# Three edits at the joint of two stages: where keys are finished, cached rows gathered, and last projections made

## What is computed

```python
# selective scan, from x_dbl = u @ x_proj_w.T
delta = softplus(delta_r @ dt_proj_w.T + dt_proj_b)
h_t = exp(delta_t * A) * h_{t-1} + (delta_t * u_t) * B_t     # per channel and state
y_t = sum_n(h_t * C_t) + u_t * D
x1  = x + y
# attention on x1
q, k = rope(rms(x1 @ Wq.T)), rope(rms(x1 @ Wk.T));  v = x1 @ Wv.T
k_blocks[blk, :, off, :], v_blocks[blk, :, off, :] = k, v    # new rows into the cache
o = softmax(mask(q @ k_all.T * SCALE)) @ v_all
```

## Time and profile before

| what | value |
|---|---|
| time, median of 3 runs | 1906.23 us (1903.25 to 1907.43) |
| span of the profiled execution, first to last instruction | 1905.3 us |
| PE busy | 1825.1 us, 96% |
| DVE busy | 1455.5 us, 76% |
| ACT busy | 1261.5 us, 66% |
| POOL busy | 1268.7 us, 67% |
| mean granted TensorE clock, share of full speed | 0.991 |

### The profile page before, as it was taken

One profiled execution on the slowest core, in us unless ns is written; L12 is line 12 of the kernel. 1 busy time (PEld: TensorE's weight loads), 2 busy tenths in 40 slices (PEclk: granted clock), 3 DMA queues, 4 the chain that ended last, 5 costly groups with the idle time before them and its releaser, 6 DMA issues.

```text
span 1905.3 us, 30000 instructions
## 1 busy us (share of the span) xinstructions
PE 1825.1 (96%) x9311; PEld 1271.2 (67%) x9311; DVE 1455.5 (76%) x2572; ACT 1261.5 (66%) x3942; POOL 1268.7 (67%) x1255
## 2 busy tenths in 40 slices
PE   6899999999999999988899899999999999999998
PEld 6777777777777777666355575756657575665764
DVE  8999999999999999999456675655657565565522
ACT  5888888888888888866356664655647465564621
POOL 5789999999999999988777654544545554450000
PEclk9999999999999999999899999999999999999999
DMA  5323323332333223321777434334343434431021
GB/s 207 146 113 146 146 96 124 146 135 107 124 147 146 111 112 143 133 78 67 227 205 216 115 103 126 106 106 129 99 127 105 117 113 111 124 89 60 30 69 38
DMA packets 117741, 230.67 MB, mean 121 GB/s; under 512 B 31364, under 2 KB 70292, under 8 KB 112464
## 3 DMA queue, kind: packets, MB, share of 16 engines
q1 hardware_dynamic: 84496, 163.48, 24.3%
q0 software_dynamic: 33088, 65.28, 12.7%
HBM read 212.09 MB, written 44.70 MB: 135 GB/s over the span
## 4 chain that ended last, share of the span: by engine, by line
PE 46%; ACT 3%; issue 1%; DVE 1%; DMA 1%; POOL 0%; ACTq 0%; DVEq 0%; SPq 0%; POOLq 0%
PE attn_psum L1974 12%; PE attn_psum L1990 12%; PE attn_psum L1904 5%; PE attn_psum L1891 4%; PE attn_psum L1884 4%; PE attn_psum L1931 3%; PE attn_psum L1875 2%; PE attn_psum L2008 2%; PE attn_psum L1865 1%; PE attn_psum L1916 1%; ACT xh L1615 1%; ACT th L1616 1%; ACT prob L1572 0%; DMA kv_at<-kv_scratch,new_now 0%; PE attn_psum L1954 0%
## 5 line engine op out<-in xcount | busy, mean ns | idle before, releaser
L1040 DVE TENSOR_TENSOR_SCAN hid<-scan_psum,dbu 128x1024 f32<-128x1024 f32 x256 | 581.8, 2273 | 1.4 <-ACT scan_psum L672 1.4
L1212 PE MATMUL scan_psum<-hid,ident 128*128 128x256 f32 x2048 | 520.3, 385 | 27.7 <-POOL hid L513 27.5
L1212 PEld LDWEIGHTS scan_psum<-hid,ident 128*128 128x128 f32 x2048 | 379.5, 191 | 189.4 <-issue 106.4
L1726 DVE CUSTOM_DVE_ANT_0 prob<-attn_psum,mask 128x336 f32<-128x336 f32 x256 | 119.8, 505 | 269.4 <-PE attn_psum L1884 269.4
L513 POOL TENSOR_TENSOR hid<-hid,kv_at 128x1024 f32<-128x1024 f32 x128 | 306.1, 2405 | 26.8 <-DVE hid L1040 26.4
L513 POOL TENSOR_TENSOR hid<-hid,bc 128x1024 f32<-128x1024 f32 x128 | 306.0, 2403 | 24.1 <-DVE hid L1040 23.6
L1578 ACT COPY p_t<-attn_psum 112x384 f32<-112x384 f32 x256 | 122.5, 487 | 274.8 <-PE attn_psum L1891 274.8
L1990 PE MATMUL attn_psum<-w,ffn_hid 128*128 128x512 f32 x512 | 238.5, 595 | 5.0 <-DVE y_sb L1791 5.0
L1504 POOL DMA_INDIRECT kv_at<-kv_scratch,new_now x189 | 200.9, 1063 | 60.8 <-issue 57.3
L1974 PE MATMUL attn_psum<-xs_in,w 128*128 128x256 f32 x1024 | 232.4, 381 | 7.5 <-ACT xs_in L1584 6.6
L672 ACT ACTIVATE scan_psum<-kv_at,neg_a 128x252 f32<-128x252 f32 x512 | 211.6, 466 | 10.7 <-DVE hid L1040 9.6
(11 more groups left out here) (229 smaller groups left out, 3034.4 us busy)
## 6 DMA issues: line engine op xcount, KB each, us to landing
bc<-bc_scratch SPq DMA_DIRECT2D x16, 2048.0 KB, 7.5
kv_at<-bc_scratch SPq DMA_DIRECT2D x15, 2048.0 KB, 7.4
q_scratch<-qg SPq DMA_DIRECT2D x32, 260.0 KB, 2.0
early<-q_scratch SPq DMA_DIRECT2D x32, 260.0 KB
x_pair<-in_x_pairs SPq DMA_DIRECT2D x32, 256.0 KB, 2.9
kv_scratch<-kvg SPq DMA_DIRECT2D x32, 256.0 KB, 2.1
a_scratch<-a_sb SPq DMA_DIRECT2D x32, 256.0 KB, 3.5
w_o<-x_scratch SPq DMA_DIRECT2D x32, 256.0 KB, 3.4
```

Of the source, the lines that this page charges most:

```text
L1040: nc.vector.tensor_tensor_scan(hid[:, k % RING, :, :].rearrange("p n t -> p (n t)"), decay[k % 2], dbu[:, k % RING, :, :].rearrange("p n t ...
L1212: mm = nc.tensor.matmul(yc, ident[:], hid[:, k % RING, i, :], start=False, stop=(k % 4 == 3 and i == 3))
```

## The change

`FETCH` lists the quarter and step at which GpSimd issues each of the nine gathers of cached rows: eight in quarters 29, 30 and 31 (two, three, three), behind the multiplication of their step, the ninth at the last step of quarter 32. The waits for the second half of the space move from the first gather to the seventh. In quarter 31 `rms` and `keys` of group 28 go from step 6 to step 7, behind the last multiplication by C. In the same quarter the projections of group 29 go eight slots (two steps) ahead on TensorE, and `take_q` on ScalarE from step 7 to step 4. The k/v projections of groups 30 and 31 are split: three of their four matmuls (chunks 0 to 2) are issued ahead of TensorE's work of the last step (`last_starts`), the fourth where all four stood.

```diff
--- before.py
+++ after.py
@@ -247,6 +247,8 @@
         C_PLACED = C_MATCH + 1 + SC
         N_ZERO = 2 + NCH
 
+        FETCH = [(4 * NT - 3, 2), (4 * NT - 3, 4), (4 * NT - 2, 1), (4 * NT - 2, 3), (4 * NT - 2, 5),
+                 (4 * NT - 1, 1), (4 * NT - 1, 3), (4 * NT - 1, 5), (4 * NT, 7)]
         LAST = [(NG - 2, 1), (NG - 1, 1), (NG - 2, 0), (NG - 1, 0)]
 
         block = ctx.enter_context(nc.Block(no_gpsimd_drain=True))
@@ -489,6 +491,7 @@
                     pool.wait_ge(dve_du, 4 * (NT - 1))
                     pool.wait_ge(act_exp, 32 * (NT - 1))
                     pool.wait_ge(pe_res, 2 * NCH * (NT - 1))
+                if n == 2 * NKC:
                     pool.wait_ge(dve_dbu, 8 * (4 * NT - 2))
                     pool.wait_ge(pool_hc, 8 * (4 * NT - 2))
                 if c == 0:
@@ -527,18 +530,16 @@
                     if k == 5:
                         for g in parts.second[1:]:
                             step(g)
+                    if (s, k) in FETCH:
+                        gather_first(FETCH.index((s, k)))
                     if k == 5 and parts.fourth:
                         if isinstance(t, int) and s == 3:
                             pool.wait_ge(c_a, 4)
                             pool.wait_ge(zero_ok, N_ZERO)
                         key_tables(s - 3)
-                    if k == 6 and parts.fourth:
+                    if k == (7 if s == 4 * NT - 1 else 6) and parts.fourth:
                         rms(s - 3, (q + 1) % 2, 16 * ((s - 3) // 2))
                         keys(s - 3, (q + 1) % 2)
-                if t == NT:
-                    for n in range(4 * q, 4 * q + 4):
-                        if n < NKC * NKV1:
-                            gather_first(n)
 
             def gather_first_new(b):
 
@@ -784,8 +785,9 @@
                             take_x(g)
                     if s == 1 and k in (2, 6):
                         cosines(k == 6)
+                    if k == (4 if s == 4 * NT - 1 else 7) and parts.third:
+                        take_q()
                     if k == 7 and parts.third:
-                        take_q()
                         query_squares(s - 2, q % 2, [0, 1])
 
                 if isinstance(t, int) and t == NT and q == 0:
@@ -1157,13 +1159,24 @@
                     if j == NCH - 1:
                         mm.then_inc((pe_q, pe_kv)[i], 1)
 
+                def last_starts():
+
+                    pe.wait_ge(act_y, NCH * 2 * NT - 1)
+                    pe.wait_ge(dve_h, 32 * NT - 1)
+                    for n, (g, i) in enumerate(LAST[0:2]):
+                        at = GRP * (g % 2)
+                        for j in range(NCH - 1):
+                            nc.tensor.matmul(last_bank[n], x1[1][:, j, at:at + GRP], w_qkv[:, j, D * i:D * i + D],
+                                             start=(j == 0), stop=False)
+
                 def last_groups():
 
                     pe.wait_ge(act_y, NCH * 2 * NT)
-                    pe.wait_ge(dve_h, 32 * NT)
                     for n, (g, i) in enumerate(LAST):
                         at = GRP * (g % 2)
-                        for j in range(NCH):
+                        if n == 2:
+                            pe.wait_ge(dve_h, 32 * NT)
+                        for j in range(NCH - 1 if i else 0, NCH):
                             mm = nc.tensor.matmul(last_bank[n], x1[1][:, j, at:at + GRP], w_qkv[:, j, D * i:D * i + D],
                                                   start=(j == 0), stop=(j == NCH - 1))
                         mm.then_inc(pe_last, 1)
@@ -1179,6 +1192,8 @@
                     last_groups()
                 for k in range(8):
                     c, b, e = 2 * (q % 2) + k // 4, q // 2, 8 * s + k
+                    if k == 7 and s == 4 * NT - 1:
+                        last_starts()
                     for i in range(4):
                         slot = 4 * k + i
                         for n, g in enumerate(parts.first):
@@ -1189,10 +1204,11 @@
                             if slot == 11 + 13 * n:
                                 project_dt(g)
                         if parts.third:
-                            if 16 <= slot < 20:
-                                project_qkv(slot - 16, 0)
-                            if 23 <= slot < 27:
-                                project_qkv(slot - 23, 1)
+                            at = 8 if s == 4 * NT - 1 else 0
+                            if 16 - at <= slot < 20 - at:
+                                project_qkv(slot - 16 + at, 0)
+                            if 23 - at <= slot < 27 - at:
+                                project_qkv(slot - 23 + at, 1)
                         if parts.scan:
                             yc = y[c % 2][:, 0:SUB]
                             if i == 0:
```

## The result

The changed kernel takes 1908.3 us in the median of 19 runs (1905.79 to 1910.38), the kernel before 1904.6 (19 runs). The ratio is 1.0019, 95% interval 1.0013 to 1.0025: 3.7 us slower, 2.5 to 4.8. The forecast was 1908.8. The profiled execution of after spans 1906.5.

What follows compares the result with a forecast made beforehand. The prediction took the joint from scan to last projections, not an engine's load, as the bound. First result 3.05 later, minus 0.4 for the store's landing, gave 2.6; 1906.2 + 2.6 = 1908.8 us, range 1904.0 to 1912.5.

Steps and rivals of the forecast that it cites:

- Gathers: Gathers moved into the scan: each costs GpSimd 1.0 to 1.3 us; a last-quarter multiplication ends 1.6 to 2.1 later.
- third rival: In the scan, a gather lasts as long as the scan instruction beside it, 2.27 us: total 1913.0; chance 0.07.
- take_q at k4: ScalarE, last quarter: waits for late q, holding the next exponentials; VectorE stalls 3.0 to 3.45 us, taken as 3.1.
- first rival: Last quarter: ScalarE not held, GpSimd on time; scan loses only 1.3 us, total 1905.3, 0.9 faster; chance 0.20.
- Keys behind the last multiplication: End of scan: last multiplication ends 0.4 us earlier, but the last x1 chunk's copy ends at 917.7, 5.65 later.
- Two parts: Split last projections on TensorE: six early matmuls cost nothing and save 2.6 us; first result still 3.05 later.
- second rival: TensorE at the scan's end drops to its lower clock, slowing early matmuls: 4.6 us later, total 1910.8; chance 0.11.
- The rest of the chain: From the first last-projection result to the last store, 915.84 to 930.66 before: nothing changes.
- Landing: Last store at the block's end: lands in 2.9 us instead of 3.3, 0.4 less.
- The sum: End of the block: 3.05 later for the first result less 0.4 for the store, 2.6 us later.
- The stage behind is taken as shifted whole: Everything after the block keeps the same waits and issue order, moved by the block's 2.6 us.

Runs made afterwards that it cites:

- keys at k7: Kernel before with one edit: group 28's key work moved behind the last multiplication by C; 1908.3 us, 1.0018 of before.
- keys at k6: Changed kernel with group 28's key work back ahead of the last multiplication by C; 1906.2 us, 1.0008 of before.
- copy first: Changed kernel with ScalarE's copy of the last x1 chunk moved ahead of take_kv; 1910.4 us, 1.0030 of before.
- own buffer: Changed kernel with a separate buffer for group 31's k/v, so its copy doesn't wait for a store; 1907.4 us, 1.0011 of before.
- one part: Changed kernel with the last k/v projections no longer split on TensorE; 1912.2 us, 1.0042 of before.
- all gathers in the tail: Changed kernel with all nine gathers of cached rows moved back behind the scan; 1908.6 us, 1.0024 of before.
- six light gathers: Kernel before with group 29's early projections, take_q at step 5, split last projections, and six gathers at scan steps with room; 1903.0 us, 0.9988 of before.
- group 30 alone early: The version with six light gathers, but only group 30's three early matmuls ahead of TensorE's last step; 1901.9 us, 0.9987 of before.

## Why the prediction was right, step by step

- **Gathers.** Priced at 1.0 to 1.3; they took 0.95 to 0.98 beside scans of 2.27. The third rival is refuted. What the Trainium skill (SBUF — State Buffer, SBUF: two separate sides) states on GpSimd's DMAs is not refuted with it: that rule is for VectorE instructions that hold the port pair shared with GpSimd, and no run here shows that the scan, with one operand in PSUM and only one in SBUF (`scan_psum,dbu`), holds it. The prediction applied the rule as if it did. The multiplication of k2 was put at 891.5 to 891.95; it ended near 890.9, in an execution 0.69 ahead: 891.6.
- **take_q at k4.** Right in place, and nearly in size. Finished q near 895.4, with the 0.69 896.0 (895.6 to 896.05 foreseen). The stall was put at 3.0 to 3.45, and the waits of the last quarter add up to 3.30. But the 0.88 among them, ahead of k3, was not foreseen: TensorE's passes at 882.78 ran at the lower level (3.09 for eight, granted clock 0.62), the copy of an x1 chunk waited for them, and the exponentials of k3 behind it. In before they ran at full speed behind the same idle time:

```profile
882.94 1.99 PE L1212 MATMUL scan_psum<-hid,ident 128*128 128x256 f32 x8 [2.05 <-POOL hid L513]
```

The version of before with the keys at k7, whose one edit acts only later, has such a wait too (0.93). In the three versions with the change's q and no wait at k3 (keys at k6, copy first, own buffer) k5 waits 2.92 to 2.96: that is the term, just under its range. Where k3 waits (0.88 in the change, 1.07 with one part), k5 waits 2.42 and 2.23, 3.30 in all both times; so the clock added about 0.35, and that the sum lies inside the range owes that much to luck. The first rival (1.3) fell; with its condition, GpSimd on time (all gathers in the tail), the gap is 1.48. Moving take_q showed the mechanism.
- **Keys behind the last multiplication.** Multiplication to 909.15 foreseen, 908.78 seen (909.47 with the 0.69); copy done at 917.7 foreseen, 917.12 seen (916.77 + 0.35; 917.81), with ScalarE's 3.62 between as read from before.
- **Two parts.** 3.05 later foreseen for the first result, 2.51 seen, 3.20 with the 0.69. The saving of 2.6 holds; that the early matmuls also keep the clock was missed. The second rival did not come in the change: after 1.78 of idle time the last projections ran at full speed.
- **The rest of the chain** is the step that failed: "From 915.84 to the last store at 930.66 nothing changes." It grew from 14.8 to 15.8. The prediction did follow group 29's keys to 921.8 and found their store hidden behind SP's loads; it did not ask who else waits for that store. ScalarE does, since group 31 reuses the buffer of group 29, and VectorE lost 0.52 to it:

```profile
924.39 0.43 DVE L998 TENSOR_TENSOR dbu<-dbu 128x256 f32<-128x256 f32 x1 [0.52 <-ACT dbu L805]
```

0.45 more went to VectorE beside the same keys.
- **Landing.** 0.4 less foreseen, 0.2 less seen (SP's wait 2.7, before 2.9).
- **The sum.** 2.6 foreseen for the block, 3.27 seen: 2.51 + 0.97 - 0.2; with the 0.69, 3.96. So the first result was put nearly right, and the chain behind it too short by 1. "The stage behind is taken as shifted whole" holds for the waits, not for the clock: the same instruction stands at 951.69 in before and at 954.05 in after, 2.36 later, and the spans differ by 1.2, since the last four records of line 2008 took 2.04 in before and their like 1.10 in after. That is the clock of one execution each; the medians differ by 3.7. That 1908.8 and 1908.3 lie only 0.5 apart is in part luck: the difference was put 1.1 too small, and the 1906.2 that it was added to, a median of three runs, stands 1.6 above the 1904.6 of 19.

## What to carry to other kernels

An engine's idle time ahead of an operation says that something can move, not that moving it pays: ask who waits for the moved work, and what stands behind that waiter in its in-order queue (take_kv behind the keys, exponentials behind take_q, a copy behind a store). A consumer placed one step too early in a queue cost about 3.0 here; the nine gathers, moved alone, cost nothing that the runs show. Work put into a gap ahead of TensorE's critical matmuls paid twice here, by its own length (2.6) and by the clock (1.8).

## What was not expected of the hardware

Two small VectorE instructions took three to four times as long beside GpSimd's keys. After, and GpSimd at the same time:

```profile
920.08 0.75 DVE L1003 TENSOR_TENSOR dbu<-sin,one_ks 128x64 f32<-128x64 f32 x1
920.94 0.63 DVE L1010 TENSOR_TENSOR dbu<-dbu 128x4 f32<-128x4 f32 x1
```

```profile
919.97 0.78 POOL L480 TENSOR_TENSOR k_n<-k_n,k_cos 128x256 f32<-128x256 f32 x1
```

In before, beside gathers, their like took 0.21 and 0.16 (917.52 and 918.31). Each ends here with a GpSimd instruction: the first at 920.83, where GpSimd goes on to the next, the second at 921.57, the next one's end (921.56). The version with the own buffer has the same 0.75 and 0.63 there. The Trainium skill (SBUF — State Buffer, SBUF: two separate sides) states that the two engines share a port pair, that a VectorE instruction with two SBUF inputs, as both are, and a GpSimd one that reads SBUF exclude each other on it, and that the first holds it to its end; the trace agrees.

And TensorE's level behind the same idle time differs between executions: after 2.04 ahead of line 1228 the eight passes took 3.25 in the version with six light gathers (827.66) and 1.99 in the one with group 30 alone early (826.59), where the two kernels do the same work up to there. So the 0.88 above belongs to the execution as much as to the kernel.
